# Padded copies of the scores' and weights' operands: blocks of four rows instead of pairs of columns

## The reference, cut to what matters

```
y = ln(x)                                     # over the last axis
qk[n,i,h,j]  = sum_c q[n,c,i,j] * k[n,c,h,j] / d
qrq[n,i,h,j] = sum_c q[n,c,i,j] * rq[c,h,i] / d        # and the same with k, rk
weight = softmax(qk + Gq * qrq + Gk * krk, axis=3)     # over j
out = sum_h weight[n,i,h,j] * Gv1 * v[n,c,h,j]
    + sum_h weight[n,i,h,j] * Gv2 * rv[c,h,i]
x = x + out;  x = x + ffn(ln(x))              # batch norm, then a sigmoid recurrence
```

## Time and profile before

| | |
|---|---|
| median of 3 runs | 140.41 us (140.3 to 140.84) |
| the profiled execution | 140.75 us; its span, first to last instruction, 139.0 us |
| mean granted TensorE clock | 0.972 |
| PE busy, share of the span | 104.0 us, 75% |
| PEld | 76.2 us, 55% |
| DVE | 92.7 us, 67% |
| ACT | 70.5 us, 51% |
| POOL | 66.7 us, 48% |

### The profile page before, as it was taken

The page is one execution under the profiler, slowest core; times in us unless marked ns, Lnnn a source line. Parts: engine busy times, 40 slices in busy tenths (PEclk is TensorE's granted clock), DMA queues, the critical chain, the costliest instruction groups (busy, mean ns, idle before and its releaser), DMA issues.

```text
span 139.0 us, 4748 instructions
## 1 busy us (share of the span) xinstructions
PE 104.0 (75%) x2078; PEld 76.2 (55%) x2080; DVE 92.7 (67%) x145; ACT 70.5 (51%) x154; POOL 66.7 (48%) x77
## 2 busy tenths in 40 slices
PE   0694995995689999990999599495886979999100
PEld 0331331284689999880989499441322438999100
DVE  5798927334030196897771069399999787889991
ACT  7957884940542456154600232424553399999200
POOL 8975855970000037628500099999965000007940
PEclk9999999999999999999599999999999999999985
DMA  4892660269100000058085000000000000000767
GB/s 146 257 282 19 151 150 1 55 136 224 50 5 5 5 5 2 5 121 188 5 190 122 5 0 5 5 5 0 0 0 0 0 0 0 5 0 17 203 185 201
DMA packets 8800, 9.56 MB, mean 69 GB/s; under 512 B 2316, under 2 KB 6412, under 8 KB 8780
## 3 DMA queue, kind: packets, MB, share of 16 engines
q1 hardware_dynamic: 8780, 9.26, 26.7%
HBM read 2.97 MB, written 2.10 MB: 36 GB/s over the span
## 4 chain that ended last, share of the span: by engine, by line
PE 29%; POOL 19%; DVE 18%; ACT 13%; issue 8%; SPq 5%; DMA 5%; POOLq 0%; ACTq 0%
PE ps L1006 9%; PE ps L1021 7%; POOL y_tile L428 6%; ACT warm L656 5%; PE ps L1042 5%; SPq L289 4%; POOL u_tile L422 4%; DVE xin L347 4%; POOL y_tile L434 4%; PE ps L1054 3%; DMA xin<-in_x_dram 3%; DVE y_tile L353 3%; PE ps L1030 3%; DVE stat L693 3%; ACT v_tile L656 2%
## 5 line engine op out<-in xcount | busy, mean ns | idle before, releaser
L403 POOL TENSOR_TENSOR att_tile<-att_tile,soft 128x1024 f32<-128x1024 f32 x4 | 7.7, 1935 | 23.9 <-DVE soft L754 23.9
L353 POOL TENSOR_TENSOR y_tile<-xin,u_tile 128x256 f32<-128x256 f32 (+1 forms) x7 | 7.1, 1046 | 20.8 <-DVE xin L347 20.8
L1006 PE MATMUL ps<-spread,u_tile 128*32 128x64 f32 x512 | 12.6, 252 | 3.9 <-issue 2.2
L1042 PE MATMUL ps<-spread,rv_t 128*32 128x128 f32 x256 | 12.0, 360 | 3.6 <-issue 3.6
L1006 PEld LDWEIGHTS ps<-spread,u_tile 128*32 128x32 f32 x512 | 12.1, 193 | 4.4 <-issue 4.4
L1042 PEld LDWEIGHTS ps<-spread,rv_t 128*32 128x32 f32 x256 | 10.9, 132 | 4.3 <-issue 3.9
L903 DVE TENSOR_SCALAR ps<-att_tile,bnv 128x512 f32<-128x512 f32 x15 | 11.0, 807 | 1.6 <-ACT warm L656 1.6
L1054 PE MATMUL ps<-spread,v_tile 128*32 128x64 f32 x512 | 9.1, 223 | 3.7 <-issue 3.7
L765 DVE TENSOR_TENSOR u_tile<-ps,xin 128x512 f32<-128x512 f32 x8 | 5.4, 687 | 8.5 <-PE ps L1042 8.2
L1114 PE MATMUL ps<-blank 128*128 128x512 bf16 x40 | 9.8, 379 | 1.5 <-DVE u_tile L796 1.3
L1054 PEld LDWEIGHTS ps<-spread,v_tile 128*32 128x32 f32 x512 | 8.5, 109 | 4.3 <-issue 4.1
(11 more groups left out here) (109 smaller groups left out, 232.4 us busy)
## 6 DMA issues: line engine op xcount, KB each, us to landing
spread<-rel_tile SPq DMA_DIRECT2D x16, 128.0 KB, 2.6
out_dram<-y_tile SPq DMA_DIRECT2D x8, 256.0 KB, 2.4
xin<-in_x_dram SPq DMA_DIRECT2D x3, 512.0 KB, 4.9
spread<-att_tile SPq DMA_DIRECT2D x12, 128.0 KB, 2.4
xin<-in_x_dram SPq DMA_DIRECT2D x2, 256.0 KB, 2.8
spread<-u_tile SPq DMA_DIRECT2D x4, 128.0 KB, 2.3
att_tile<-in_L_conv_rv_dram SPq DMA_DIRECT2D x4, 128.0 KB, 2.6
att_tile<-in_L_conv_rq_dram SPq DMA_DIRECT2D x1, 128.0 KB, 6.3
```

Of the source, the lines that this page charges most:

```text
L353: return eng.tensor_tensor(result[:, :, rows, :], back[:, at:at + P * k].rearrange("p (q i j) -> p q i j", q=Q, i=k), x2[:, :, rows, :], A ...
L1006: return nc.tensor.matmul(ps[group(q), first + j // 8, at:at + G * HALF].rearrange("p (g i) -> p g i", g=G), u[:, q, :, j], y_bd[:, q, :, ...
L1042: ins = nc.tensor.matmul(bank(4 + n % 4)[group(g), P * k:P * (k + 1)].rearrange("p (q jp t) -> p q jp t", q=Q, t=RUN), rv_t[:, ROWS * n + ...
```

## The change

The unit of the padded copy becomes a block of four rows. Element (i, j) of an image stands at 128 * (i div 4) + 4 * j + (i mod 4). Four rows of one column are adjacent (16 bytes), such groups are 512 bytes apart for the next four rows, and a row's elements are 16 bytes apart. The turned copies are written by one instruction of 1024 elements each, where two of 512 stood: `turn_y` four times, `weigh` twice on POOL and twice on DVE. The semaphores count accordingly. The DMAs move the same pieces, and the matmuls have the same shapes, weights and order.

```diff
-        y_bd = spread4[:, :, :, :].rearrange("p q g (b jp i t) -> p q g b jp i t", b=2, i=HALF, t=RUN)
-        att_bd = spread4[:, :, :, :].rearrange("p g q (b jp i t) -> p g q b jp i t", b=2, i=HALF, t=RUN)
+        y_bd = spread4[:, :, :, :].rearrange("p q g (b j k) -> p q g b j k", b=PIECES4, j=C)
+        att_bd = spread4[:, :, :, :].rearrange("p g q (b j k) -> p g q b j k", b=PIECES4, j=C)
...
-        turned_att = rel_tile[:, :].rearrange("p (x g jp i t) -> p x g i jp t", x=CHUNKS, g=2, i=HALF, t=RUN)
+        turned_att = rel_tile[:, :].rearrange("p (x m j k) -> p x m k j", x=CHUNKS, j=C, k=ROWS)
...
-        def in_pairs(t):
-            return t.rearrange("p (b jp i t) -> p b i jp t", b=2, i=HALF, t=RUN)
-
-        def by_pairs(t):
-            return t.rearrange("p i (jp t) -> p i jp t", t=RUN)
+        def turned(t):
+            return t.rearrange("p (b j k) -> p b k j", b=PIECES4, j=C)
+
+        def by_blocks(t):
+            return t.rearrange("p (b k) j -> p b k j", k=ROWS)
 
         def recip_of(n):
-            return soft[:, 1, n // 2, HALF * (n % 2):HALF * (n % 2 + 1)].unsqueeze(2).unsqueeze(3).broadcast_to([P, HALF, C // RUN, RUN])
+            return soft[:, 1, n, :].rearrange("p (b k) -> p b k", k=ROWS).unsqueeze(3).broadcast_to([P, PIECES4, ROWS, C])
+
+        def rows_of(half):
+            return slice(PIECES4 // 2 * half, PIECES4 // 2 * (half + 1))
 
         def wait_weights(eng, n):
 
-            eng.wait_ge(S["weights_dve" if n % 2 else "weights"], 2 * (n // 2 + 1))
+            eng.wait_ge(S["weights_dve" if n % 2 else "weights"], n // 2 + 1)
...
-                sp.wait_ge(S["y_turned_act"], 2 * (q + 1))
+                sp.wait_ge(S["y_turned_act"], q + 1)
...
             def weigh(n):
                 pool.wait_ge(S["weight_recip"], n + 1)
-                for g in range(2):
-                    nc.gpsimd.tensor_tensor(turned_att[:, n, g, :, :, :], by_pairs(att[:, n, g, :, :]), recip_of(2 * n + g), ALU.mult
-                                            ).then_inc(S["weights"], 1)
+                nc.gpsimd.tensor_tensor(turned_att[:, n, :, :, :], by_blocks(att_m[:, n, :, :]), recip_of(n), ALU.mult
+                                        ).then_inc(S["weights"], 1)
...
-                for b in range(2):
-                    nc.scalar.copy(in_pairs(turned_y[q])[:, b], by_pairs(y[:, q, HALF * b:HALF * (b + 1), :])).then_inc(S["y_turned_act"], 1)
+                nc.scalar.copy(turned(turned_y[q]), by_blocks(y[:, q, :, :])).then_inc(S["y_turned_act"], 1)
...
-                return nc.tensor.matmul(ps[group(q), first + j // 8, at:at + G * HALF].rearrange("p (g i) -> p g i", g=G),
-                                        u[:, q, :, j], y_bd[:, q, :, half, j // RUN, :, j % RUN],
+                return nc.tensor.matmul(ps[group(q), first + j // 8, at:at + G * HALF].rearrange("p (g b k) -> p g b k", g=G, k=ROWS),
+                                        u[:, q, :, j], y_bd[:, q, :, rows_of(half), j, :],
...
-                        ins = nc.tensor.matmul(side_bank(n)[group(q), P * k:P * (k + 1)].rearrange("p (g jp t) -> p g jp t", g=G, t=RUN),
-                                               r_fac[:, ROWS * n + k, :], y_bd[:, q, :, n // 4, :, ROWS * (n % 4) + k, :],
+                        ins = nc.tensor.matmul(side_bank(n)[group(q), P * k:P * (k + 1)].rearrange("p (g j) -> p g j", g=G),
+                                               r_fac[:, ROWS * n + k, :], y_bd[:, q, :, n, :, k],
...
-                        ins = nc.tensor.matmul(bank(4 + n % 4)[group(g), P * k:P * (k + 1)].rearrange("p (q jp t) -> p q jp t", q=Q, t=RUN),
-                                               rv_t[:, ROWS * n + k, :], att_bd[:, g, :, half, :, row + k, :],
+                        ins = nc.tensor.matmul(bank(4 + n % 4)[group(g), P * k:P * (k + 1)].rearrange("p (q j) -> p q j", q=Q),
+                                               rv_t[:, ROWS * n + k, :], att_bd[:, g, :, n, :, k],
...
-                        ins = nc.tensor.matmul(ps[group(g), first + j // 8, at:at + Q * HALF].rearrange("p (q i) -> p q i", q=Q),
-                                               v_t[:, j, g, :], att_bd[:, g, :, half, j // RUN, :, j % RUN],
+                        ins = nc.tensor.matmul(ps[group(g), first + j // 8, at:at + Q * HALF].rearrange("p (q b k) -> p q b k", q=Q, k=ROWS),
+                                               v_t[:, j, g, :], att_bd[:, g, :, rows_of(half), j, :],
```

More of the change, by code:

```diff
@@ L20 @@
 CHUNKS = 4
-RUN = 2
 WARM = 9
@@ L769, in weigh @@
                 dve.wait_ge(S["weight_recip"], n + 1)
-                for g in range(2):
-                    nc.vector.tensor_tensor(turned_att[:, n, g, :, :, :], by_pairs(att[:, n, g, :, :]), recip_of(2 * n + g), ALU.mult
-                                            ).then_inc(S["weights_dve"], 1)
+                nc.vector.tensor_tensor(turned_att[:, n, :, :, :], by_blocks(att_m[:, n, :, :]), recip_of(n), ALU.mult
+                                        ).then_inc(S["weights_dve"], 1)
             score_add(0)
@@ L1034, in relative_values @@
             def relative_values(n):
-                half, row = n // 4, ROWS * (n % 4)
                 if n < 4:
```

## The result

The change made the kernel slower: 148.49 us as the median of 4 runs (148.29 to 148.61), against 140.62 us for 4 runs of before (140.3 to 140.97). The ratio is 1.0558, with a 95% interval of 1.0525 to 1.059. That is 7.9 us; the forecast was +2.5, and 148.49 lies outside of the range of 137.8 to 148.0. The profiled execution took 148.61 us at a clock of 0.971, against 140.75 at 0.972, so the clock has no part in it. In the experiments further down a median is that of all runs, while a ratio leaves out the profiled execution and the runs more than 1.5% above the fastest of the others.

The account below looks back on a forecast made before the run. No single engine bounds it: turned copies first, then PE's reading and instruction supply, then POOL's list. Merging gave -0.4, dearer relative reads +2.1 at step (1); total +2.5 on the profiled 140.75, median 143.0, range 137.8 to 148.0.

Parts of the forecast that it names:

- The sign and the price of the relative reads: PE's relative scores and values: single elements 16 bytes apart cost 57.3 ns per record against 40.8, making the kernel slower.
- reads as now: Rival: PE's relative reads cost the same as before, leaving only the merging's -0.4, 140.0 us; chance 0.16.
- free neighbouring lines: Rival: PE reads elements 16 bytes apart like adjacent ones, so instruction blocks bound the relative part; -2.4, 138.0 us; chance 0.19.
- a price of 64 ns and more: Rival: PE's four streams share a price per line; 145 us at 64 ns per record, 152 at 81.6; chance 0.16.
- Step (1) of the sum: Relative scores, pieces 0 to 3: 128 records take 7.3 us for 5.2; with -0.4 the relative values start at 68.0.
- It holds if writing elements 16 bytes apart is free: Condition of the merged copies' -0.4: `turn_y(0)` 0.12, `turn_y(2)` 0.12 and `weigh(0)` 0.16 us saved.
- dear writes: Rival: ACT writes single elements at its read price, each `turn_y` 2.07 us; 146 with the forecast's reads; chance 0.17.
- Scores and weighted sums at zero: PE's reads in runs of 16 bytes there change nothing; a gain of up to 1.5 us would be off the chain.
- Steps (2) and (3): First 128 relative values take 7.3 us for 6.0; the last sums' block starts at 81.0 for 78.56, +2.5.
- my rule of a fixed 3.7 us: PE's instruction supply: a block of 256 takes at least 3.7 us when the one before took no longer.
- Step (4): POOL's list after the sums is unchanged; PE's second half ends 4.3 later, with 2.1 of room, total +2.5.

Follow-up runs that it names:

- the probe: Kernel before with a different read pattern in each of eight relative pieces and each quarter of the first scores, DVE row sums beside them; one execution, 143.62 us.
- the padded kernel: The change with blocks of two rows, each followed by 2 unused elements, so pairs are 264 bytes apart; 138.56 us, ratio 0.9744 to before.

## Why the prediction was right and wrong

**The sign and the price of the relative reads: right, the price in part by luck.** 57.3 ns per record were taken from ACT's strided read, and 59.1 were measured, and 59.0 to 59.4 in five more profiles. But that row of ACT reads elements 128 bytes apart, and at that distance PE pays 75 in the probe: the price of one engine at one distance happened to be near that of another at 16 bytes. That the old pairs and the new singles both leave the adjacent pattern was no reason for "reads as now"; the probe shows that being alone in a line is a price of its own. The rivals of free neighbouring lines (138) and of a price of 64 ns and more (145, 152) are out by this row.

**Step (1) of the sum, "Pieces 0 to 3 of the relative scores ... +2.1 at 48.12": the step that failed.** It followed the data: the first half needs only four pieces. It did not follow ACT's queue, in which all eight `rel_out` copies stand ahead of `score_exp(0)`. In before this cost next to nothing, since POOL's subtraction ended at 52.70 (50.75 + 1.95) and the exponential started at 53.02. With slower pieces it costs the other four as well: +2.3 at DVE's addition, as forecast, and +4.6 at the exponential. Moving one copy behind the exponential gave 1.8 to 1.9 us of this back at the exponential, and 1.4 to 1.8 at the relative values.

**"It holds if writing elements 16 bytes apart is free": it wasn't.** The term was taken at -0.4. ACT's copy took the 2.04 us that the text had as its other end (2.07), and the rival with "dear writes", at 146 with my reads, had the mechanism. `turn_y` took some 0.87 more each (2.04 for 1.17), and `turn_y(3)`, which the forecast had off the path, came onto it. At the issue of the last DMA this was 1.05 us, its landing added 1.95 that are not shown to be the copies' doing, and what reached the relative scores of both was 1.2. Writes alone cost 1.2 to 1.6% of the time. I gave this the chance 0.17 because pairs write for free; pairs use each line twice and singles 16 bytes apart don't, the very rule that I had weighed for the reads. It was not applied to the writes.

**Scores and weighted sums at zero: no difference that these runs can tell** (1.0363 with the relative reads alone, 1.0405 with all).

**Steps (2) and (3), values and blocks: +0.8 forecast from the values' start to the last sums, nothing found.** From the start of the values to the last block of the first sums it is 12.24 us in before, 12.19 in the change and 12.20 in the padded kernel, although 128 records of values take 6.38, 7.62 and 6.11 of it. The supply of instructions sets this length, and my rule of a fixed 3.7 us after the block before was too strict: in the change the 123 records of sums ahead of the block in between take 1.96 us at 15.9 ns, so PE entered that block at 83.1 and found the next at 85.99, 2.9 later. In other runs with the dear reads the length was up to 13.0, but it was 13.05 and 13.03 with the writes alone too, where the reads are those of before; what decides it is open.

**Step (4), POOL's list unchanged and enough room for PE's second half: nearly.** `centre(0)` now waited 0.62 us for DVE's sum, of an addition that had waited for the second half's values: +0.4. Behind it the list runs as in before.

The account of the profiled 7.9: input 0.8, ACT's copies and the last landing 1.2, relative pieces 4.7 (2.3 of them behind ACT's queue), from the exponential to the values 0.8, from there to the sums -0.1, `centre(0)` 0.4 and the rest 0.1. Of the last four, the dearer `weigh` (2.28 for 2.11, and DVE's 2.97 and 1.99) is a likely part of the 0.8: from the start of `weigh(0)` to SP's first issue it is 2.31 us for 2.13, and 2.38 to 2.62 in the four other profiles with this write. The rest of the 0.8 no run isolates.

## What to carry to other kernels

Before a time is taken off or put on a wait, read what stands ahead of the waiting instruction in its engine's own list: data that is early does not help an engine that is queued behind data that is late. A layout has a price at each place that touches it, so hold every pattern, the writes too, against the same rule: here a float32 element should share its 16-byte line with another one that is accessed with it, and the distance of PE's runs should not be 128 or 256 bytes. When a merged instruction is worth 0.1 us and a doubled access price 0.9, the merge is a small term beside the new stride.

## What the runs showed of the hardware that I had not expected

- A read pattern of PE can slow the other engines: beside pairs 256 bytes apart, POOL's operation took 7.28 us for 1.94, DVE's 3.80 for 1.22 and ACT's 3.72 for 0.59. At 264 bytes these operations were back at 2.04, 1.24 and 0.66. The Trainium skill (SBUF — State Buffer, Terms) gives PE and ACT ports of their own; by these rows that doesn't keep ACT from being slowed beside PE's reads, and where they meet isn't shown.
- Writes have the price of reads: 1024 elements written 8 bytes apart took 1.14 us on ACT, and 2.04 when 16 bytes apart. POOL hardly notices (1.92 to 1.95 and 2.08 to 2.28).
- Relative values that took 7.62 us in place of 6.38 did not move the start of the last sums' block away from that of the values (12.19 and 12.24 us), since this block was held by its instructions and not by data (0.82 us of idle time marked "issue" ahead of it).
- A DMA of 128 KB, the last padded copy of y, landed in 2.37 to 2.46 us in half of the profiles and in 3.50 to 4.32 in the other half, whichever kernel ran.
